# A diffusion step and a deformable convolution: a written-out schedule, and a gather table that holds each pixel pair once

## The reference

```
h = D*(c0*h0 - 2E*h + cm_x*roll(h,1,W) + cp_x*roll(h,-1,W) + cm_y*roll(h,1,C) + cp_y*roll(h,-1,C)) + 2*DT*D*fsrc
```

## Time and profile before

| what | value |
|---|---|
| median of 3 runs | 857.23 us (856.39 to 858.77) |
| the profiled execution | 856.12 us, span of its trace 854.3 us |
| busy: PE, PEld, DVE | 740.4 (87%), 551.5 (65%), 527.2 us (62%) |
| busy: ACT, GpSimd | 203.8 (24%), 549.8 us (64%) |
| mean granted TensorE clock | 0.924 |
| gathers: software queue q0 | 75.53 MB |

### The profile page before, as it was taken

The page is one execution under the profiler, slowest core; times in us unless marked ns, Lnnn a source line. Parts: engine busy times, 40 slices in busy tenths (PEclk is TensorE's granted clock), DMA queues, the critical chain, the costliest instruction groups (busy, mean ns, idle before and its releaser), DMA issues. The chain is left out here.

```text
span 854.3 us, 10727 instructions
## 1 busy us (share of the span) xinstructions
PE 740.4 (87%) x4130; PEld 551.5 (65%) x4130; DVE 527.2 (62%) x772; ACT 203.8 (24%) x401; POOL 549.8 (64%) x589
## 2 busy tenths in 40 slices
PE   5979979999999899989999999899999985764655
PEld 3545646677777677776777777677777664654544
DVE  5466558667775878657956795777767764422221
ACT  3302502151125212411333222411252001100000
POOL 1000037777777777777777777777777777777772
PEclk8999979999999999999999999999999998856565
DMA  6200033335333533353335333353335333533331
GB/s 192 67 16 1 15 81 107 106 106 159 113 107 102 163 113 106 103 163 107 110 107 154 115 113 105 114 153 111 105 106 162 111 105 106 162 112 106 107 111 46
DMA packets 53404, 92.83 MB, mean 109 GB/s; under 512 B 12313, under 2 KB 33641, under 8 KB 53353
## 3 DMA queue, kind: packets, MB, share of 16 engines
q0 software_dynamic: 27648, 75.53, 30.3%
q1 hardware_dynamic: 25704, 16.61, 7.2%
HBM read 79.70 MB, written 12.40 MB: 108 GB/s over the span
## 5 line engine op out<-in xcount | busy, mean ns | idle before, releaser
L392 POOL DMA_INDIRECT pixels<-table,index x576 | 546.7, 949 | 288.9 <-issue 175.2
L623 DVE TENSOR_TENSOR weighted<-pixels,banks 128x2304 f32<-128x2304 f32 x64 | 163.4, 2553 | 158.5 <-DMA pixels<-table,index 145.5
L799 PE MATMUL banks<-prod,const 128*128 128x448 f32 (+2 forms) x720 | 217.5, 441 | 15.9 <-DVE prod L543 15.9
L802 PE MATMUL banks<-const,weighted 128*128 128x128 f32 x1280 | 185.4, 298 | 44.4 <-DVE weighted L623 26.6
L802 PEld LDWEIGHTS banks<-const,weighted 128*128 128x128 f32 x1280 | 162.3, 157 | 70.8 <-ACT sampled_T L732 30.6
L799 PEld LDWEIGHTS banks<-prod,const 128*128 128x128 f32 x720 | 116.1, 195 | 90.9 <-issue 90.2
L732 ACT ACTIVATE sampled_T<-banks 128x512 f32<-128x512 f32 (+1 forms) x128 | 56.0, 437 | 334.7 <-PE banks L802 334.7
L543 DVE TENSOR_TENSOR prod<-coef,banks 128x1024 f32<-128x1024 f32 x80 | 95.5, 1215 | 51.7 <-PE banks L799 51.6
L799 PE MATMUL banks<-filt,sampled_T 128*128 128x64 f32 x640 | 89.2, 290 | 14.4 <-ACT sampled_T L732 7.9
L799 PEld LDWEIGHTS banks<-filt,sampled_T 128*128 128x128 f32 x640 | 83.1, 205 | 25.5 <-ACT sampled_T L732 17.2
L799 PE MATMUL banks<-conv_w,xT 128*128 128x384 f32 (+1 forms) x384 | 85.9, 380 | 0.0
(11 more groups left out here) (97 smaller groups left out, 477.5 us busy)
## 6 DMA issues: line engine op xcount, KB each, us to landing
pixels<-table,index POOLq DMA_INDIRECT x576, 2.8
table<-xn SPq DMA_DIRECT2D x48, 128.0 KB
table<-xn SPq DMA_DIRECT2D x16, 144.0 KB
x<-x_in SPq DMA_DIRECT2D x32, 64.0 KB, 2.1
out_dram<-x SPq DMA_DIRECT2D x64, 32.0 KB
table<-corner_w SPq DMA_DIRECT2D x16, 70.0 KB
const<-const_in SPq DMA_DIRECT2D x1, 768.0 KB, 5.6
table<-corner_w SPq DMA_DIRECT2D x8, 62.0 KB
```

The source lines that it names most:

```text
L392: pool.indirect_dma_start(out=pixels[:, col % NB, k, :], out_offset=None, in_=table[0:(u + 1) * TY * TX, :], in_offset=bass.IndirectOffset ...
L623: dve.tensor_tensor(weighted[:, col % 2, :, 0:K2, :].rearrange("p q k c -> p k q c"), pixels[:, col % NB, :, :].rearrange("p k (q c) -> p ...
L799: return pe.matmul(dst, lhsT, rhs, start=start, stop=stop, skip_group_check=True)
L802: return pe.matmul(dst, data, moved, start=start, stop=stop, is_transpose=True, skip_group_check=True)
```

## The change

The table holds each pair once. Its rows are 512 bytes, the pair (y, x), (y, x+1), and the rows of a column lie behind each other: row (x * 35 + y) is followed by (x * 35 + y + 1). A gather still brings each partition 1 KB, now beginning at any 512 byte row. An image is written with 4 DMAs, and the borders are cleared with 5.

The orders of the engines are written out piece by piece for all 8 images (`DVE_PIECES`, `ACT_PIECES`, `PE_PIECES`). Image 0 goes alone for a while; image 1's pieces come in during its last steps, and the first column's multiply stands in image 1's fourth step. Within a step but the first, the own product now goes first. The rest of the restructuring:

- `ones` is set by DVE instead of loaded; sides 2 and 3 of image 0 are loaded from ACT's queue; `warm_up` issues products of `ones` with itself whose result nobody reads, 8 ahead of the first sum, 10 behind it and 9 behind the first squares' sum.
- Gates are made one gate at a time for all 8 columns, in three parts by row shift (`conv0a`, `conv0b`, `conv0`), each of which waits only for its own copy of the rows; the batch-norm parameters of the gates are folded into the taps, 2 values per partition. Products: 36 an image instead of 24, in columns of 64 to 256 instead of 128 and 384.
- `gate_terms` is split into `force`, `dgx`, `dgy`, and `coefficients` into `coefx`, `coefy`. For images after the first, the own sums wait for both gate products and the force term.
- Group-norm and row buffers exist twice (`xc`, `squares`, `gvar`, `xT`), some others share memory.
- For image 0, `edges1` and `own` have bank 6, so `gy` and `gx` need not wait for `edges1`.
- SP writes the table of image u + 1 ahead of both stores of image u.
- The very last column is fetched and multiplied in taps 0 to 5, 6 to 7 and 8; the last three of the group's columns are added apart from the fourth, whose stores are split over SP and ACT.

The diff, cut to its core:

```diff
+PAIR = 2 * C
+ROWS = B * TX * TY
+ROW_ORDER = (1, 0, 2)
-TABLE_DMAS = 2 * SIDES
+TABLE_DMAS, CLEARINGS = SIDES, 5
+LAST_TAPS = ((0, 6), (6, 8), (8, K2))
+WARM_UP = (8, 10, 9)
+DVE_PIECES = """
+mean1+0 bnp+0 var1+0 scale1+0 cells+0 edges1+0 bnout+0 den+0 diff+0 dgx+0 coefx+0 force+0 dgy+0 seed0+0 px0+0
+coefy+0 py0+0 coef0+0 prod0+0 seed1+0 prod1+0 px1+0 py1+0 seed2+0 prod2+0 px2+0 py2+0 seed3+0 prod3+0 px3+0
+py3+0 mean1+1 seed4+0 prod4+0 px4+0 var1+1 py4+0 scale1+1 final1+0 edges1+1 final2+0 mean2+0 var2+0 scale2+0
+den+1 edges2+0 samp1+0 diff+1 dgx+1 samp2+0 coefx+1 dgy+1 force+1 seed0+1 px0+1 coefy+1 py0+1 coef0+1 prod0+1
...
+PE_PIECES = """
+sum1+0 sq1+0 turn+0 gy+0 gx+0 conv0a+0 conv0b+0 conv0+0 conv1a+0 conv1b+0 conv1+0 init+0 edge+0 own+0 stx0+0
+sty0+0 sto0+0 sto1+0 stx1+0 sty1+0 sto2+0 stx2+0 sty2+0 sto3+0 sum1+1 stx3+0 sty3+0 sq1+1 sto4+0 stx4+0 sty4+0
+turn+1 shift+0 sum2+0 conv0a+1 sq2+0 gx+1 gy+1 conv0b+1 halo+0 turn2+0 conv0+1 off+0 conv1a+1 conv1b+1 conv1+1
+init+1 edge+1 own+1 stx0+1 sty0+1 sto0+1 sto1+1 stx1+1 sty1+1 sto2+1 stx2+1 sty2+1 sto3+1 stx3+1 sty3+1 flip0@0
...
-FIRST_FILLS = {"conv1": [("conv1", 4, "act", "gate1")]}
+FIRST_FILLS = {"turn": [("main1", 5, "act", "main1"), ("edges1", 6, "dve", "edges1")],
+               "conv1": [("conv1", 4, "act", "gate1")],
+               "own": [("own", 6, "dve", "coef0")]}
...
-    table = nc.dram_tensor("table", [ENTRIES, ENTRY], f32, kind="Internal").ap()
+    table = nc.dram_tensor("table", [ROWS + 1, PAIR], f32, kind="Internal").ap()
...
-                    for k in range(2):
-                        sp.dma_start(table_y[u, LO - k:LO - k + H, at:at + count,
-                                             k * 2 * C:(k + 1) * 2 * C], pairs).then_inc(s_table, 16)
+                    sp.dma_start(table_x[u, at:at + count, LO:LO + H, :].rearrange("x y e -> y x e"), pairs)\
+                      .then_inc(s_table, 16)
...
-                            out=pixels[:, col % NB, k, :], out_offset=None, in_=table[0:(u + 1) * TY * TX, :],
+                            out=pixels[:, col % NB, k, :], out_offset=None, in_=corners(u),
...
-                seq(dve.scalar_tensor_tensor(wk(entry), wo(lo)[:, :, 0:K2], float(TX), wo(lo)[:, :, K2:2 * K2],
+                seq(dve.scalar_tensor_tensor(wk(entry), wo(lo)[:, :, K2:2 * K2], float(TY), wo(lo)[:, :, 0:K2],
...
+            def warm_up(n):
+                for i in range(n):
+                    mm(banks[:, 6, 0:P], ones[:, :], ones[:, :], True, True)
...
+            def depthwise(u, g, i):
+                dst = bank(u, f"conv{g}")
+                if i == 0:
+                    wait_bank_empty(u, f"conv{g}")
+                    mm(wc(dst), ones[:, :], every_col(shift_w[:, g, :], WS), True)
+                moved_rows(u, 1, i)
+                dh = ROW_ORDER[i]
+                ins = spread(dst, xT[:, 0, dh, :], conv_w[:, g, dh, :], SLOT_ORDER, C, WS, i == 2)
+                if i == 2:
+                    ins.then_inc(s_full, 1)
...
+                if u:
+                    pe.wait_ge(s_gated, 2 * u + 2)
+                    pe.wait_ge(s_force, u + 1)
...
+                for a, b in LAST_TAPS if col == LAST else ((0, K2),):
+                    if a == 0:
+                        dve.wait_ge(s_pixels[col % NB], (col // NB) * 16 * K2 + 16 * b)
+                    else:
+                        dve.wait_ge(arrived(col, a), 16 * (b - a))
+                    if b == K2 and col == LAST:
+                        add_columns(u, WS - COLS, COLS - 1)
```

More of the change, by code:

```diff
@@ L54 @@
[L54 to L74, removed]
-            else:
-                name, _, i = token.partition("@")
-                per_image = GROUPS_U if name == "add" else WS
-                n, count = u * per_image + int(i), UNITS * per_image
-            if 0 <= n < count:
-                pieces.append((name, n))
-    return pieces
@@ new lines @@
+stx3+2 sty3+2 flip0@9 sto4+2 flip1@9 sum1+3 flip0@10 filt@9 stx4+2 sty4+2 flip1@10 shift+2 sq1+3 sum2+2 flip0@11
+filt@10 sq2+2 turn+3 flip1@11 gx+3 halo+2 conv0a+3 flip0@12 filt@11 turn2+2 gy+3 conv0b+3 off+2 conv0+3 flip1@12
+conv1a+3 flip0@13 filt@12 conv1b+3 conv1+3 flip1@13 init+3 flip0@14 filt@13 edge+3 own+3 stx0+3 sty0+3 flip1@14
+flip0@15 filt@14 sto0+3 flip1@15 sto1+3 stx1+3 sty1+3 flip0@16 filt@15 sto2+3 flip1@16 stx2+3 sty2+3 filt@16
+sto3+3 stx3+3 sty3+3 flip0@17 sto4+3 flip1@17 sum1+4 flip0@18 filt@17 stx4+3 sty4+3 flip1@18 shift+3 sq1+4
@@ new lines @@
+conv0b+5 off+4 conv0+5 flip1@28 conv1a+5 flip0@29 filt@28 conv1b+5 conv1+5 flip1@29 init+5 flip0@30 filt@29
+edge+5 own+5 stx0+5 sty0+5 flip1@30 flip0@31 filt@30 sto0+5 flip1@31 sto1+5 stx1+5 sty1+5 flip0@32 filt@31
+sto2+5 flip1@32 stx2+5 sty2+5 filt@32 sto3+5 stx3+5 sty3+5 flip0@33 sto4+5 flip1@33 sum1+6 flip0@34 filt@33
+stx4+5 sty4+5 flip1@34 shift+5 sq1+6 sum2+5 flip0@35 filt@34 sq2+5 turn+6 flip1@35 gx+6 halo+5 conv0a+6 flip0@36
+filt@35 turn2+5 gy+6 conv0b+6 off+5 conv0+6 flip1@36 conv1a+6 flip0@37 filt@36 conv1b+6 conv1+6 flip1@37 init+6
@@ new lines @@
+flip0@38 filt@37 edge+6 own+6 stx0+6 sty0+6 flip1@38 flip0@39 filt@38 sto0+6 flip1@39 sto1+6 stx1+6 sty1+6
+flip0@40 filt@39 sto2+6 flip1@40 stx2+6 sty2+6 filt@40 sto3+6 stx3+6 sty3+6 flip0@41 sto4+6 flip1@41 sum1+7
+flip0@42 filt@41 stx4+6 sty4+6 flip1@42 shift+6 sq1+7 sum2+6 flip0@43 filt@42 sq2+6 turn+7 flip1@43 gx+7 halo+6
+conv0a+7 flip0@44 filt@43 turn2+6 gy+7 conv0b+7 off+6 conv0+7 flip1@44 conv1a+7 flip0@45 filt@44 conv1b+7
+conv1+7 flip1@45 init+7 flip0@46 filt@45 edge+7 own+7 stx0+7 sty0+7 flip1@46 flip0@47 filt@46 sto0+7 flip1@47
@@ L434, in scale @@
[L434 to L439 removed]
+                i = which - 1
```

600 lines of the change are left out of this document (376 added, 224 removed).

## The result

The changed kernel's median is 829.51 us in 4 runs (825.84 to 831.08), beside 857.2 for the kernel before: a ratio of 0.967 (0.963 to 0.971). The profiled execution took 827.97 us with a span of 826.1; the one before took 856.12, so 28.15 us are to be found.

A forecast was written before the change was run, and what follows sets the result against it. GpSimd's gathers bound the kernel, between the wait for image 0's indices and the tail. Terms 0 + 6 + 5.5 + 1.6 + 6.5 + 0 + 5 - 1.5 = 23.1 off 856.12 gave 833.0 profiled, 834 median; range 823 to 850.

The forecast's parts named there:

- up to xn: Image 0's start up to the normalised image: no gain taken (0), ends 1 us either way.
- turn to own sums: Image 0's gradients and depthwise convolutions: 6 us gained, 2 with the clock low, at best 7.
- own sums to the second step's product: Image 0, own sums to first h: seed and products made beside the own sums gain 5.5 us, ends 3 and 6.5.
- steps 2 to 5: Image 0's later steps: image 1's turn, gx and one sum leave them, gaining 1.6 us, ends 0 and 2.5.
- h to the index: Image 0 from h to its index: less of image 1's work stands ahead, gaining 6.5 us, ends 3 and 8.
- gathers: GpSimd's 576 gathers: cost as today despite the new table rows, gain 0.
- between: Between first and last gather: image 1's later index and PE's queue charged with a 1.5 us loss.
- tail: Behind the last gather: split last column, earlier turns and fewer stores per queue gain 5 us, ends 3.5 and 7.6.
- rival 4: GpSimd's gathers cost more for their two rows; fully doubled, 1379 us; chance 0.03.
- rival 1: Later images' indices are late, 2 us of gap at each of 7 images: 848 us; chance 0.15.
- Rival 3: PE becomes the bound and the kernel slower; at 95 us an image, 867 us; chance 0.03.
- Rival 2: Clock and step gains fail: warm-ups don't hold it, first step and later steps don't shrink: 841 us; chance 0.14.

## Why the prediction was right, step by step

The forecast was 834 and 829.5 came out, 4.5 us faster. The mechanism held where it carries the result: GpSimd's gathers are the bound and don't change, and the gain is made ahead of the first and behind the last. In one term, the steps, it was wrong, in another the clock was put down to one cause of two, and the terms were mostly too small; the first gather came at 93.81, just outside my 94 to 104. By the profiled executions:

| step | forecast | measured | from |
|---|---|---|---|
| up to xn | 0 | -0.3 | turn 12.22, now 12.49 |
| turn to own sums | 6 | 6.8 | own sums 40.09, now 33.59 |
| own sums to the second step's product | 5.5 | 6.0 | 15.3, now 42.87 - 33.59 = 9.3 |
| steps 2 to 5 | 1.6 | 3.3 | 28.7, now 68.20 - 42.87 = 25.3 |
| h to the index | 6.5 | 7.8 | 32.4, now 92.74 - 68.20 = 24.5 |
| gathers, and "between" | -1.5 | -0.7 | 720.9, now 721.6 |
| tail | 5 | 5.2 | 15.9, now 10.7 |

**Gradients and convolutions, 6.** The size was nearly right (the path that I had added up, 21 against 27.9, even gives 6.9), its reason partly wrong. I gave 4.1 us to the warm-ups and treated gy's wait as another matter. The clock did give 4.2 (9.95 us for gy and gx, now 5.76), but the runs show 1.6 us for the warm-ups alone and 3.8 for the bank, each with a share of the clock: it is at 1.00 only where the warm-ups are there and nothing waits from the turn on. The narrow products cost what I said: 5.99 us for 36 records against 5.37 for 24, 1.2 us for two gates where I had 1.4. The ACT and DVE chain behind gx did hide, since no wait stands ahead of the own sums.

**Own sums to the second step, 5.5.** As forecast, the first step runs straight behind the own sums, at full clock (5.19). That the init and DVE's products beside the own sums do it is read from the trace; no run undoes them.

**Steps 2 to 5, 1.6: the step that failed.** I wrote that own first "only moves PE's order, as its x part still waits for 0.7 + 1.2 of DVE", and made a step 6.65. It takes 6.17 (42.87 to 49.04). PE starts on the own product as soon as that is there, at 43.71, and runs its 5.29 us unbroken, since px is ready (43.48 + 1.2 = 44.7) when the own product's two records are through. What remains per step is 0.87 us of standing still, not the 1.41 of the earlier trace rows; 4 x 0.5 us is what my sum left out. The kernel before has the same step without image 1's work in it, the fifth. Its first products in the timeline:

```profile
77.46 2.35 DVE L543 TENSOR_TENSOR prod<-coef,banks 128x1024 f32<-128x1024 f32 x2 [2.81 <-PE banks L799]
```

From there to 84.04 are 6.58 us. So own first takes 0.41 us off each step, 1.6 in all, and the other 1.7 of the 3.3 is image 1's work that no longer stands between the steps (2.3 us, now 0.7). This is read from the traces; no run has the old order alone.

**h to the index, 6.5.** Each station came a little ahead of my count (halo 14.9 us behind h, not 15.6; index written at 24.7, not 26). Most of it is that I added whole durations of TensorE's blocks, though the next one starts 0.1 to 0.2 us before the one ahead ends (81.17 + 2.12 = 83.29, and halo starts at 83.13). That TensorE's order is what counts here is shown by the run with halo ahead of gy: another 2.2 us from moving products alone.

**The gathers, 0, and rival 4.** Source rows don't matter. The page has 48 packets a gather as before, the gather takes 0.950 us, and the new table in the kernel before measured 0.9999. The Trainium skill (DMA: Bandwidth & Descriptors, on the limit of descriptors per engine) gives one descriptor per contiguous run of the last dimension; read by source rows it would have meant 256 runs and up to 1379 us, and these traces disagree with that reading. That section is about DMAs issued from SP or ACT, and these are GpSimd's. How a gather is cut the packets don't show (48 and 32 for 128 indices); the time shows that an index may point at a 1 KB run over two rows at no cost.

**Between, -1.5, and rivals 1 and 3.** Image 1's list was needed at 93.81 + 90.35 = 184.2 and was there at 178.5, 5.6 us ahead, where I counted 2. No stall came of it: the 1.5 us that I charged was nothing, and the 0.7 in the table is the gathers' own time. So rival 1 (848) didn't come. Rival 3 is real but 4 products away: two more an image are still free, four cost 3.5 us. Per image TensorE's steady pace is 89.8 us against the gathers' 90.3. I put the threshold at 93.6 us an image, and that was the point where the whole gain is gone; the first loss begins much sooner, as soon as the deficits of the five intervals from image 1 to image 6 exceed image 1's margin.

**Rival 2**, the clock and the step gains failing, was wrong in all its parts: a granted clock of 1.00 in 12 to 26 us, 5.19 for the first step, and steps that shrank by 3.3 us.

**The tail, 5.** The early turns carry it, as the undivided column shows. That it came out at 5.2 is in part luck: I took 2.2 us for the 16 turns, and they took 3.34, at a granted clock of 0.54, while the filter ahead of them took 1.33 and not the 2.40 that I had used; the same kernel again had a tail of 8.8 us, which would be a gain of 7.1.

## What to carry to other kernels

Where an in-order engine issues without a gap, the time is what lies ahead of its first instruction plus what lies behind its last; shorten those two ends, and check that every later list is still in time, since each microsecond won at the start is also asked of image 1. A wait on TensorE can cost twice, once itself and once through the clock of what follows, so a free buffer that removes a wait was worth more here than dummy products (3.8 against 1.6 us). Take the share of an engine in the chain of waits with care when two engines have almost the same pace.

## What the hardware did that I had not expected

**DVE stood still beside a GpSimd memset.** In the run with 512 byte gathers, `pixels` is cleared once on GpSimd, 11.6 us that I had thought hidden. The timeline:

```profile
5.58 11.62 POOL L477 MEMSET pixels<- 128x13824 f32 x1
...
6.92 0.69 DVE L514 TENSOR_TENSOR p_arr<-x,banks 128x512 f32<-128x512 f32 x1
7.52 9.72 DVE L563 TENSOR_SCALAR bn<-bn 128x64 f32<-128x64 f32 x1
7.62 9.62 DVE L541 RECIPROCAL gate_scale<-gate_scale 128x2 f32<-128x2 f32 x1
```

An operation on 64 values a partition took 9.72 us, where the changed kernel takes 0.19 for it; it ends at 17.24, just behind the memset's 17.20. The larger one ahead of it, which reads PSUM, took its usual 0.69 beside the same memset. Behind the two in DVE's queue stands the work on the variance, which so starts at 18.70 and not at 9.93. Of these 8.8 us some 8.1 are the standstill; 0.7 is a first sum that was slow in this run. The other 1.5 of the 10.3 us by which the first gather is late come behind it: the turn, gy and gx take longer, at a granted clock of 0.79 in 20 to 30 us. A small case of it is in the changed kernel (a tensor_scalar on 2 values takes 1.33 us and ends at 5.11, as the memset of `xT` ends at 5.10). The Trainium skill (SBUF — State Buffer, "Who interferes with whom") says that DVE in its two-port mode and GpSimd fully block each other, whoever issues first; the trace agrees with that, though it doesn't show the mode in which an operation ran.

**More work made a list earlier.** Two useless products per image brought image 1's index 2.8 us forward, because the granted clock of 97 to 104 us went from 0.75 to 1.00.

**A gather's time doesn't follow its bytes.** 512 bytes a partition instead of 1 KB changed its pitch from 1.2549 to 1.2500 us, and other runs with 1 KB have 1.2523.
